# Four-row compression of prepared tiles moved from TensorE to DMAs and GpSimd, and feed-forward products placed among the next tile's turns

## The reference, cut to what matters

```python
x  = hidden_states                       # 4 x 1024 x 512
xn = layernorm(x)
q  = rope(rmsnorm(xn @ Wq + bq));  lk = rope(rmsnorm(xn @ Wlk + blk));  lv = xn @ Wlv + blv    # 16 heads of 128
w_cmp   = softmax((xn @ Wcmp + bcmp) in groups of four rows)
entries = sum over the four rows of w_cmp * xn          # 256 x 512 in each batch
ck = rope(rmsnorm(entries @ Wk + bk));  cv = entries @ Wv + bv
sparse = softmax over the 8 best of q . ck, times cv;   local = softmax of a 128-row band of q . lk, times lv
out = x + ((sparse + local) / 2) @ Wo + bo + fp8(xn / 2) * 2 @ fp8(W2 / 2) * 2
```

## Time and profile before

| | |
|---|---|
| median of 3 runs | 2492.66 us (2492.33 to 2492.68) |
| profiled execution, first to last instruction | 2492.2 us |
| median of the runs beyond that span | 0.5 us |
| mean granted TensorE clock | 1.000 |
| busy: PE, PEld | 99 %, 88 % |
| busy: DVE, POOL, ACT | 80 %, 70 %, 67 % |
| step of a unit, 256 of them in 2492 us | 9.7 us on average |

### The profile page before, as it was taken

How to read it: one execution, slowest core, us unless ns; L and a number is a source line. 1 busy time by engine, 2 the same in 40 slices (tenths; PEclk the granted TensorE clock), 3 DMA queues, 4 the chain that set the end, 5 groups by cost and what they waited for, 6 DMA issues and landing times. The chain is left out here.

```text
span 2492.2 us, 56206 instructions
## 1 busy us (share of the span) xinstructions
PE 2462.4 (99%) x15574; PEld 2190.6 (88%) x15606; DVE 1996.7 (80%) x6637; ACT 1675.3 (67%) x4866; POOL 1749.7 (70%) x3150
## 2 busy tenths in 40 slices
PE   7999999999999999999999999999999999999998
PEld 6888888888888988888888889888888888888887
DVE  7788888888778887787777888887878878888786
ACT  5667777767666677667666666767676666666665
POOL 6787787776786666666677766666667767676674
PEclk9999999999999999999999999999999999999999
DMA  5433233333332122121441221221235213212301
GB/s 159 136 107 113 71 109 115 117 109 117 123 119 82 52 90 90 60 90 43 151 150 53 81 82 60 90 86 64 78 124 166 94 59 100 75 61 94 98 10 52
DMA packets 183530, 232.36 MB, mean 93 GB/s; under 512 B 19762, under 2 KB 101172, under 8 KB 183220
## 3 DMA queue, kind: packets, MB, share of 16 engines
q1 hardware_dynamic: 182644, 228.50, 28.3%
q10 hardware_dynamic: 576, 0.26, 0.1%
HBM read 162.64 MB, written 65.01 MB: 91 GB/s over the span
## 5 line engine op out<-in xcount | busy, mean ns | idle before, releaser
L1598 POOL TENSOR_TENSOR t<-raw,tB 128x128 f32<-128x128 f32 x512 | 226.4, 464 | 593.8 <-DVE raw L1167 593.7
L987 ACT ACTIVATE ch<-bVC,blT 128x128 fp32r<-128x128 f32 x512 | 160.5, 365 | 511.1 <-PE bVC L726 511.1
L631 PE MATMUL bQK<-wh,xh 128*128 128x512 f32 x1024 | 424.4, 414 | 0.0
L632 PE MATMUL bQK<-wl,xh 128*128 128x512 f32 x1024 | 403.8, 394 | 0.0
L633 PE MATMUL bQK<-wh,xl 128*128 128x512 f32 x1024 | 401.4, 392 | 0.0
L1542 POOL TENSOR_TENSOR r<-ss,mh 128x4 f32<-128x4 f32 x256 | 286.4, 1119 | 60.1 <-DVE ss L1175 57.5
L647 PE MATMUL bVC<-wh,xh 128*128 128x256 f32 x1024 | 310.0, 303 | 0.0
L954 ACT ACTIVATE P<-P,nm,r 128x256 f32<-128x256 f32 (+1 forms) x512 | 295.3, 583 | 0.0
L1203 DVE CUSTOM_DVE_ANT_0 P<-bS,cst 128x256 f32<-128x256 f32 (+1 forms) x512 | 204.2, 399 | 110.5 <-PE bS L679 106.1
L649 PE MATMUL bVC<-wh,xl 128*128 128x256 f32 x1024 | 289.4, 283 | 0.0
L648 PE MATMUL bVC<-wl,xh 128*128 128x256 f32 x1024 | 289.0, 282 | 0.0
(11 more groups left out here) (188 smaller groups left out, 7617.9 us busy)
## 6 DMA issues: line engine op xcount, KB each, us to landing
wh<-kept SPq DMA_DIRECT2D x144, 256.0 KB, 4.1
wl<-kept SPq DMA_DIRECT2D x144, 256.0 KB, 4.6
kept<-wh SPq DMA_DIRECT2D x48, 256.0 KB, 3.2
kept<-wl SPq DMA_DIRECT2D x48, 256.0 KB, 3.4
woh<-kepto SPq DMA_DIRECT2D x48, 256.0 KB, 3.2
wol<-kepto SPq DMA_DIRECT2D x48, 256.0 KB, 3.7
ini<-in_hidden_states SPq DMA_DIRECT2D x24, 256.0 KB, 4.5
xs<-xsh SPq DMA_DIRECT2D x24, 256.0 KB, 2.5
```

The source lines that it names most:

```text
L631: e.matmul(bQK[:, :], a, b, start=kt == 0, stop=False)
L632: e.matmul(bQK[:, :], a, bl, start=False, stop=False)
L1598: last = e.tensor_tensor(t2[:, :, :, d_], raw[:, u % 2, :, :, s_], tB[:, :, u % 8, d_].unsqueeze(1).broadcast_to([128, 2, 2, 32]), ALU.mult)
```

## The change

For tiles 8 to 31:

- `logits` and `entries` on PE, `diagonal`, `exp_w` and `put_et` on ACT, `group_max` and `weights4` on DVE are no longer issued.
- `spread` (SP) writes the tile's 128 logits to DRAM and reads them back as 32 rows of four; `below_max` (DVE), `exp_4` (ACT) and `shares` (DVE) form the softmax on 32x4 elements; `give` (SP) writes the weights to DRAM and reads them back as one row of 128 in all partitions.
- POOL joins the turned tile's high and low part (`whole_x`, 128x512), multiplies it by the weights (`weigh`, 128x512) and adds fours of neighbours (`fold`, 256 and 128 elements a partition) into `et`. These follow the tile's base by 4, 6 and 7 steps, behind `normalise_p` in POOL's list.
- `ckv` and what follows move one step later from block 2 on; the second `new_ck` of a batch and its doubling too.
- The feed-forward product of tile `t` moves to the step in which tile `t+1` is turned; `turn_ffn` issues the four turns and the four products in turns, ahead of the scores. Tiles 23 and 31 keep `ffn` by itself, one step later.
- `XR`, the number of `xt` buffers, goes from 4 to 3.

```diff
-XR, QR = 4, 2
+XR, QR = 3, 2
...
-        "max": (2, 2, 3), "ew": (3, 3, 4), "wm": (3, 3, 4), "et": (3, 4, 8), "park": (3, 3, 4)}
-
-BLOCK_LAGS = {"kv": (4, 5, 7), "put": (4, 5, 7), "rope": (4, 5, 7), "turn": (6, 6, 9), "hi": (6, 6, 9), "lo": (6, 6, 9)}
+        "max": (2, 2, None), "ew": (3, 3, None), "wm": (3, 3, None), "et": (3, 4, None), "park": (None, None, 4),
+        "spread": (None, None, 2), "below": (None, None, 3), "share": (None, None, 4), "give": (None, None, 5),
+        "whole": (None, None, 4), "weigh": (None, None, 6), "fold": (None, None, 7)}
+
+BLOCK_LAGS = {"kv": (4, 5, 8), "put": (4, 5, 8), "rope": (4, 5, 8), "turn": (6, 6, 10), "hi": (6, 6, 10), "lo": (6, 6, 10)}
...
-    return 64 * (NB - 1) + 2 + 7 * t // 2 if t < NL else tile_base(t) + 5
+    if t < NL:
+        return 64 * (NB - 1) + 2 + 7 * t // 2
+    return tile_base(t) + 6 if t % 8 == 7 else tile_base(t + 1)
...
+            def spread(t):
+                n = t - FIRST_TILES
+                e.wait_ge(S["wl"], t + 1)
+                e.dma_start(spread_l[t].rearrange("(p a) -> p a", a=1), smt[:, t % 2, 2:3]).then_inc(S["d_g0"], 16)
...
+                e.dma_start(l4, spread_l[t].rearrange("(g r) -> g r", r=4)).then_inc(S["d_g1"], 16)
+
+            def give(t):
+                n = t - FIRST_TILES
+                e.wait_ge(S["wq"], 2 * n + 2)
+                e.dma_start(spread_w[t].rearrange("(g r) -> g r", r=4), w4).then_inc(S["d_g2"], 16)
...
+                e.dma_start(wide[:, :], bc(spread_w[t], 128)).then_inc(S["d_g3"], 16)
...
-            def entries_ffn(t, f):
-
-                e.wait_ge(S["wm"], t + 1)
+            def turn_ffn(t, f):
+
+                e.wait_ge(S["xn"], t + 1)
                 e.wait_ge(S[free["T"][0]], free["T"][1])
                 e.wait_ge(S["q8"], 4 + ffn_pos(f) + 1)
                 e.wait_ge(S[free["Y"][0]], free["Y"][1])
                 for kt in range(KT):
                     c = slice(kt * 128, (kt + 1) * 128)
-                    m = e.matmul(entries_of(t)[:, kt * 32:(kt + 1) * 32], xt[:, t % XR, c], wm[:, :], start=True, stop=True)
+                    m = e.transpose(bT[:, c], xt[:, t % XR, c], ident)
                     if kt == KT - 1:
-                        m.then_inc(S["et"], 1)
+                        m.then_inc(S["xt"], 1)
                     last = e.matmul(bY[:, :], q8[:, ffn_pos(f) % QR, c], w2q[:, kt, :], start=kt == 0, stop=kt == KT - 1)
                 last.then_inc(S["ff"], 1)
-                free["T"] = ("put_et", t + 1)
+                free["T"] = ("lo_x", t + 1)
                 free["Y"] = ("init", ffn_pos(f) + 1)
...
+            def below_max(t):
+                n = t - FIRST_TILES
+                e.wait_ge(S["d_g1"], 16 * (n + 1))
+                e.tensor_reduce(top4, l4, mybir.AxisListType.X, ALU.max).then_inc(S["lm"], 1)
...
+            def whole_x(t):
+                e.wait_ge(S["lo_x"], t + 1)
+                e.tensor_tensor(xf[:, :, :], f32(xsh[:, :, :]), f32(xsl[:, :, :]), ALU.add).then_inc(S["xf"], 1)
+
+            def weigh(t):
+                n = t - FIRST_TILES
+                e.wait_ge(S["xf"], 3 * n + 1)
+                e.wait_ge(S["d_g3"], 16 * (n + 1))
+                w = wide[:, :].unsqueeze(1).broadcast_to([128, KT, 128])
+                e.tensor_tensor(xf[:, :, :], xf[:, :, :], w, ALU.mult).then_inc(S["xf"], 1)
+
+            def fold(t):
...
+                e.tensor_tensor(x4[:, :, 0:2], x4[:, :, 0:2], x4[:, :, 2:4], ALU.add).then_inc(S["xf"], 1)
...
+                e.tensor_tensor(et[:, :, (t % 4) * 32:(t % 4 + 1) * 32], x2[:, :, :, 0], x2[:, :, :, 1],
+                                ALU.add).then_inc(S["put_et"], 1)
```

More of the change, by code:

```diff
@@ L264, in build @@
         wrow = P[:, 1, 0, 0:256]
+        l4, e4, w4 = wm[0:32, 0:4], wm[0:32, 4:8], wm[0:32, 12:16]
+        top4, sum4, inv4 = wm[0:32, 8:9], wm[0:32, 9:10], wm[0:32, 10:11]
+        junke = eg[:, :, :].rearrange("p a b -> p (a b)").bitcast(BF16)[:, 0:512]
+        wide = dg
         bQK = ps("bQK", [128, 512])
@@ L594, in run_sync @@
                     load_ini(t)
+                if tile_at(s, "give") is not None:
+                    give(tile_at(s, "give"))
+                if tile_at(s, "spread") is not None:
+                    spread(tile_at(s, "spread"))
             for u in range(NU - 7, NU):
@@ L841, in run_tensor @@
                     fill(8)
-                if tile_at(s, "turn") is not None:
+                beside = tile_at(s, "turn") is not None and ffn_at(s, 3) is not None
+                if beside:
+                    turn_ffn(tile_at(s, "turn"), ffn_at(s, 3))
+                elif tile_at(s, "turn") is not None:
                     turn_x(tile_at(s, "turn"))
@@ L859, in run_tensor @@
                     values(u4, 1)
-                if tile_at(s, "turn") is not None:
-                    logits(tile_at(s, "turn"))
+                if tile_at(s, "max") is not None:
+                    logits(tile_at(s, "max"))
                 if u0 is not None:
@@ L1094, in run_scalar @@
                     exp_w(tile_at(s, "ew"))
+                if tile_at(s, "share") is not None:
+                    exp_4(tile_at(s, "share"))
                 if block_at(s, "hi") is not None:
@@ L1127, in run_scalar @@
                         hi_wo(q)
-                if tile_at(s, "norm") is not None:
+                if tile_at(s, "norm") is not None and tile_at(s, "norm") < FIRST_TILES:
                     diagonal(tile_at(s, "norm"))
@@ L1458, in run_vector @@
                     group_max(tile_at(s, "max"))
+                if tile_at(s, "below") is not None:
+                    below_max(tile_at(s, "below"))
                 if u0 is not None:
@@ L1484, in run_vector @@
                     weights4(tile_at(s, "wm"))
+                if tile_at(s, "share") is not None:
+                    shares(tile_at(s, "share"))
                 if block_at(s, "rope") is not None:
@@ L1679, in run_gpsimd @@
                     rope_rest(u0)
-                if u2 is not None and u2 >= 64 and u2 % 64 == 2:
+                if u2 is not None and u2 >= 64 and u2 % 64 == 3:
                     new_ck(u2 // 64, 1)
@@ L1705, in run_gpsimd @@
                     power_x(tile_at(s, "power"))
+                if tile_at(s, "whole") is not None:
+                    whole_x(tile_at(s, "whole"))
+                if tile_at(s, "weigh") is not None:
+                    weigh(tile_at(s, "weigh"))
+                if tile_at(s, "fold") is not None:
+                    fold(tile_at(s, "fold"))
                 if s >= 0:
```

115 lines of the change are left out of this document (72 added, 43 removed), and 4 rows, old and new, of the table SIGNALS.

## The result

The changed kernel takes **2559.1 us** (median of four runs, 2554.1 to 2567.7) against 2492.7 for the kernel before it: 1.0269 times as long, with a 95 % interval of 1.0252 to 1.0286. The forecast was 2488.7, within 2480 to 2498. It is 66 us slower, and the forecast missed it by 70. The profiled execution took 2554.1 us; its span is 2552.3 us, 60.1 more than before. The four runs lie further apart than those of the kernel before (2492.3 to 2492.8), and the mean granted clock goes with them: 0.991 in the one of 2554.1 us, 0.986 in the one of 2567.7.

What follows compares the result with a forecast made beforehand. PE's list of products was taken as the bound: -23.7 us of work, +9.3 and +6.4 of waits at `ckv`, +4.0 of smaller waits, sum -4.0. That gave a 2488.2 us span and a 2488.7 us median, range 2480 to 2498.

Steps and rivals of the forecast that it cites:

- Costing nothing: SP's `spread` and `give` transfers, ACT's list and three `xt` buffers: claimed to add no time.
- Work off PE: PE's list loses logits products (5.3 us), sums alone (8.9) and sums beside products (9.5): 23.7 us saved, range 21.9 to 28.1.
- The four pairs: In `turn_ffn` on PE, four turns alternating with four feed-forward products: priced at 1.18 us, against 1.31 apart.
- Odd blocks: PE at `ckv` of blocks 3, 5 and 7 waits for POOL's `fold`: about 3.1 us each, 9.3 in all.
- Blocks 4 and 6: PE at `ckv` of these blocks waits for DVE's `init` to free the bank: 3.2 us each, 6.4 in all.
- Smaller waits: PE waiting on later DVE and POOL work, in steps 82, 146, 125, 189 and 15 to 64: 4.0 us, range 0 to 15.
- the five stands: PE's forecast standstills at `ckv`: three in odd blocks, two in blocks 4 and 6, 15.7 us together.
- The clock falls: Rival: each of five PE standstills over 3 us lowers the clock, losing 3.5 us each; 2506 us, chance 0.06.
- The waits are short: Rival: DVE's and POOL's lateness is absorbed and PE's five standstills are a third shorter; 2479.5 us, chance 0.26.
- DVE becomes the bound: Rival: DVE binds around each tile, small waits on PE reach 15 us; 2499.7 us, chance 0.12.
- Slower: Outcome class for the whole kernel: slower than before by over 0.2 %, chance 0.12.

Runs made afterwards that it cites:

- e5: Changed kernel with the DRAM transfers of `spread` and `give` made for tile 8 only, later tiles' left out: 2520.4 us, 38.7 less than changed.
- e11: Changed kernel with logits turned on DVE before the write, `below_max` at DVE's step end, `ckv` a step later, feed-forward products alone: 2483.8 us, 0.9961 of the kernel before.
- e7: Changed kernel with transfers for the first tile only, `ckv` one step later and feed-forward products alone: 2482.7 us, 0.9953 of the kernel before.
- e3: Changed kernel with the logits written as 32 partitions x 16 B instead of 128 x 4 B, sums weighed by wrong logits: 2535.0 us.
- e10: Changed kernel with the logits turned on DVE and written as four rows of 128 B: 2525.4 us, 33.7 less than changed.
- e2: Changed kernel with SP issuing the write of the logits first in its step instead of last: 2588.0 us, 29 slower than changed.
- e9: Changed kernel with `below_max` at the end of DVE's step and `exp_4` after the exponentials of ACT's next step: 2540.8 us, 18.3 less.
- e6: Changed kernel with all four transfers of `spread` and `give` in ACT's list instead of SP's: 2597.1 us, 1.0420 of the kernel before.

## Why the prediction was wrong

**The step that failed** is "Costing nothing: the DMAs of `spread` and `give` have a whole step before they are read (the longest wait for one on SP is a few us ...); what they hold up on SP is prefetch." They cost 38.7 us (e5); once they are mended no cost of theirs shows (e11 beside e7). Three parts of it were false. The length: I took the rows of large transfers for a write of 128 single words, which takes 7.0 us and not a few (e3, e10: 24 and 34 us come back with the shape alone). The start: I placed the issue at the end of `normalise`; for tiles 10, 11, 14, 19 and 27 SP came 12.5, 7.2, 11.3, 7.5 and 7.5 us later (the 9 to 13 in e2's expectation is too high), since its list is in order and stood behind the splits on POOL and DVE for the first three and behind a wait for PE for the last two (`fetch_w`). These are the five places where DVE waited. For 17 of the other 19 tiles SP came within 0.03 us, for tiles 9 and 13 after 1.4 and 2.2, and DVE did not wait. I asked when an engine comes to its work at each wait on PE and never of SP. The place of the reader: `below_max` stands in front of `put_qk`, so DVE waits with everything behind it (e9: 18 us).

**Work off PE, -23.7.** Slightly too much. The four pairs take 1.29 us and not 1.18. That is about as long as turns and products take apart (1.31), and with 1.31 the sum is 21.9 us, the lower end of my range. Two other figures agree with it: the account above, and e7, where PE is busy for 2441.6 us against 2462.4 with 3.4 us at the lower clock, so for 22.5 us less.

**Odd blocks, 3.1 us each.** Right: 2.68, 3.66 and 3.66 by `et`. `fold` was priced at 0.74 + 0.46 and takes 0.70 + 0.42. POOL's timeline behind `ckv` of block 7:

```profile
1935.61 0.61 POOL L1713 TENSOR_TENSOR xf<-xf 128x256 f32<-128x256 f32 x1
1936.29 0.41 POOL L1717 TENSOR_TENSOR et<-xf 128x128 f32<-128x128 f32 x1
```

```profile
1936.76 3.78 PE L830 MATMUL bY<-wkv,et 128*128 128x256 f32 x8 [3.66 <-POOL et L1717]
```

**Blocks 4 and 6, 3.2 us each.** Right: 2.96 each.

```profile
1056.30 1.97 PE L830 MATMUL bY<-wkv,et 128*128 128x256 f32 x8 [2.96 <-DVE ini L1415]
```

**Smaller waits, 4.0 us.** Too small, the second step that failed. In e5, which has no transfers past the first tile, PE is idle for 36.5 us more than before; 15.9 of it are the five stands ahead of `ckv`, so 20.6 are smaller waits. Those of `turn_ffn` alone are 10.4 us, ten of the twelve for `q8`, which the sum does not name: I asked when the bank came free and when `add_out` ended, and not who makes the products' operand. `add_out` was late as feared, but 1.95 us and in steps 90 and 154, not 0.6 in steps 125 and 189.

**The rivals.** "The clock falls" had 0.06 and a price of 3.5 us for each of five stands. It fell at three of these five: for 3.4, 3.4 and 10.2 us, half of which is 8.5 us. The same eight passes of `ckv` took 1.97 us at the upper level (1056.30) and 3.78 at the lower (1936.76). It also fell at four places that the forecast did not know. In e5 it fell at four of the five. The Trainium skill (TensorE: Matmul & The Clock Gate, Why this matters for your kernels), named there, warned of such gaps, and the trace now agrees, with 44.2 us at 0.50. I had weighed the rule by the longest wait of a trace that had none to show: 1.7 us without a fall bounds nothing at 3. The sign that I gave for it, `PEclk` leaving 9 on the page, stayed silent all the same, since the stretches are too short for the slices. One reading of the forecast the trace does not bear out as a clock: it put the 634 ns of the earlier trace rows to the lower level, but the windows of that opening (30 to 38 us of the kernel before) have a granted clock of 1.00. The eight passes there take 3.54 us, as long as in the later stretches at 0.50; why the clock's record differs is not shown. "The waits are short" fell: the five stands were not a third shorter. "DVE becomes the bound" fell: DVE is busy for 78 %; it was late, not full. Slower had 0.12 in all.

**The sum again.** 2488.7, with 38.7 for the transfers, 16.6 more for the smaller waits, 10.2 for the lower clock that is left in e5 (half of 20.5), 1.8 for the pairs and 0.2 for `ckv`'s stands, is 2556.2 us, by an estimate from these traces; measured were 2559.1. The costs that were left out or weighed too low all had the same sign, and I had treated each as small on its own.

## What to carry to other kernels

- Moving work off the bounding engine buys what it takes off the list only if each value still arrives in time. Ask of each new edge four things: when its issuer comes to it in its own list, how long it takes in this very shape, what stands behind the reader, and, for a moved product, who makes each operand.
- A wait in an in-order queue can't be moved to a "free" engine: SP's head (e2) and ACT (e6) were both worse than SP's end. Shorten the wait instead (e10). And see what is issued right behind a slow transfer: it lands late with it (e2).
- What a fix is worth depends on what stands beside it: the same pair of edits gave 26.4 us beside the slow write and 37.7 without the transfers, and the place of `below_max` gave 18.3 beside the slow write and nothing beside the short one. Measure fixes on a base where the largest cost is gone.
- Read the granted clock in windows of some 10 us around each new wait; the page's 40 slices can hide it.

## What the runs showed of the hardware

- A write from SBUF to DRAM of 512 bytes, issued from SP, took 7.0 us as 128 x 4 B, 2.0 as 32 x 16 B, and 1.5 as 4 x 128 B, on average of 24 (waits of SP behind the issue). With fetches of 256 KB right behind the first, the DMA engines moved 27 GB/s at a busy share of 0.97, and the fetches landed some 12 us after their issue (e2). On ACT's queue the 128 x 4 B write was waited for up to 5.9 us.
- In the changed kernel the granted clock went to the lower level around stands of PE of 8.00, 2.68 and 3.66 us, but not at two of 2.96. In e5 it fell at the same two places (2.96 and 2.95 us) and not at the first (2.72). In the changed kernel it fell behind stands of 1.29 and 1.59 us that lie 4 us apart (991.96, 995.84), and not behind 1.99 and 1.59 (1618.12, 1622.00). In e11 it fell after 2.14 us, once. The length of the last stand alone does not decide. Windows of PE in e11:

```profile
440.00:462.00 22.00, 21.59 (x132) 1.00 0.21 61
465.00:468.00 3.00, 3.00 (x8) 0.50 0.84 263
```

- Turns of 128 columns (f32) and products of 512 columns (bf16) alternate at 0.33 us a pair (915.63 to 916.61 in the changed kernel is three pairs), which is 0.11 + 0.22, what they take apart: alternating hides nothing and loses nothing.
- Adding fours of neighbours on POOL with strided reads cost no more than contiguous operations of that size: 698 ns for 256 elements, 420 for 128, against 737 for 256 in the earlier trace rows.
